# A new order inside each build step of a four-layer GNN kernel: one-hots, weighting, lots and stores

## What is computed

```python
# layer 0
Wh = h @ W + b
sim = dot(Wh[row], Wh[col]) / max(|Wh[row]| * |Wh[col]|, EPS)
base = adj_v * softplus(deg_coeff[0] * deg_v + deg_coeff[1]) * (row != col)
prop_pos = segment_sum((base * relu(sim))[:, None] * Wh[col], row)
prop_neg = segment_sum((base * -relu(-sim))[:, None] * Wh[col], row)
x = x + scale * (coeff[0] * prop_pos + coeff[1] * prop_neg + coeff[2] * Wh)
# layers 1 to 3: LightGCN with three hops, GIN, gated mean over the neighbours
```

## Time and profile before

| what | us |
|---|---|
| median of the three runs | 1067.99 |
| the profiled execution, its own time | 1059.61 |
| its span in the trace | 1057.9 |
| mean granted TensorE clock, share of full | 0.943 |
| VectorE busy | 854.9 (81%) |
| TensorE matmuls busy | 840.5 (79%) |
| ScalarE busy | 619.2 (59%) |
| TensorE busy in the 33.00 us from 500 to 533 us | 26.33 |

### The profile page before, as it was taken

The page is one execution under the profiler, slowest core; times in us unless marked ns, Lnnn a source line. Parts: engine busy times, 40 slices in busy tenths (PEclk is TensorE's granted clock), DMA queues, the critical chain, the costliest instruction groups (busy, mean ns, idle before and its releaser), DMA issues. The chain is left out here.

```text
span 1057.9 us, 33568 instructions
## 1 busy us (share of the span) xinstructions
PE 840.5 (79%) x14240; PEld 593.2 (56%) x14240; DVE 854.9 (81%) x1214; ACT 619.2 (59%) x2090; POOL 175.8 (17%) x364
## 2 busy tenths in 40 slices
PE   0695558878787878878778787744999998999997
PEld 0362435544445545455444554424999998996653
DVE  8986778878888888888888888656666798587896
ACT  0764447767767777677776767617999942112000
POOL 4815711112111121111211112100000000000000
PEclk9987569999999999999999999976999999998999
DMA  9933116566666667666675666759700000783893
GB/s 210 232 115 86 54 41 155 136 151 161 153 139 147 147 165 160 139 147 150 165 157 135 150 144 161 164 159 391 302 2 2 2 2 1 307 310 130 323 388 128
DMA packets 44697, 164.32 MB, mean 155 GB/s; under 512 B 14245, under 2 KB 16375, under 8 KB 40823
## 3 DMA queue, kind: packets, MB, share of 16 engines
q1 hardware_dynamic: 33990, 133.22, 42.6%
q0 software_dynamic: 8288, 27.59, 12.8%
q10 hardware_dynamic: 2256, 1.23, 0.5%
HBM read 78.63 MB, written 63.72 MB: 135 GB/s over the span
## 5 line engine op out<-in xcount | busy, mean ns | idle before, releaser
L1170 PE MATMUL b_ps<-b_mv,b_soh 64*128 64x50 bf16 (+1 forms) x9600 | 192.3, 189 | 119.9 <-DVE b_mv L1055 66.4
L1170 PEld LDWEIGHTS b_ps<-b_mv,b_soh 64*128 64x128 bf16 x9600 | 164.2, 95 | 171.9 <-DVE b_mv L1055 110.9
L1390 PE MATMUL layers_ps<-layers_u,layers_c 128*128 128x192 bf16 x2500 | 210.9, 247 | 11.4 <-ACT layers_u L1572 8.8
L1390 PEld LDWEIGHTS layers_ps<-layers_u,layers_c 128*128 128x128 bf16 x2500 | 208.0, 98 | 16.5 <-DVE layers_y L1696 8.0
L946 ACT ACTIVATE b_c_row<-b_ps 128x300 bf16<-128x300 f32 (+1 forms) x275 | 119.7, 435 | 79.5 <-PE b_ps L1170 72.6
L1093 DVE TENSOR_TENSOR b_y<-b_sim,b_ps 128x512 f32<-128x512 f32 (+1 forms) x175 | 109.9, 628 | 63.9 <-PE b_ps L1224 59.3
L964 ACT ACTIVATE b_pos<-b_ps,k_coef 128x1024 f32<-128x1024 f32 x100 | 92.8, 928 | 91.9 <-PE b_ps L1170 90.7
L1055 DVE TENSOR_TENSOR b_mv<-b_mv,b_parts 128x2808 bf16<-128x2808 bf16 x100 | 145.6, 1456 | 0.0
L1581 ACT ACTIVATE k_passed<-layers_c 128x128 bf16<-128x128 bf16 x450 | 131.4, 294 | 0.0
L1051 DVE TENSOR_TENSOR b_soh<-k_numbers,b_bits 128x2304 bf16<-128x2304 bf16 x100 | 121.9, 1219 | 0.0
L1082 DVE SCALAR_TENSOR_TENSOR b_sim<-b_ps,k_coef,b_pos 128x1024 f32<-128x1024 f32 x100 | 104.6, 1046 | 16.6 <-ACT b_pos L964 16.6
(11 more groups left out here) (275 smaller groups left out, 1123.4 us busy)
## 6 DMA issues: line engine op xcount, KB each, us to landing
layers_c<-g_blocks SPq DMA_DIRECT2D x25, 1600.0 KB, 9.2
g_blocks<-b_g_row SPq DMA_DIRECT2D x52, 400.0 KB
c_blocks<-b_c_row SPq DMA_DIRECT2D x25, 800.0 KB
g_blocks<-head_odd SPq DMA_DIRECT2D x48, 400.0 KB
layers_c<-c_blocks SPq DMA_DIRECT2D x12, 1600.0 KB, 26.3
k_passed<-b_sent POOLq DMA_DIRECT2D x24, 768.0 KB, 6.5
prep_attr<-in_edge_attr SPq DMA_DIRECT2D x2, 1883.0 KB
prep_attr<-in_edge_attr SPq DMA_DIRECT2D x1, 1876.0 KB
```

Of the source, the lines that this page charges most:

```text
L1170: return nc.tensor.matmul(out, lhsT, rhs, start=start, stop=True, skip_group_check=True)
L1390: return nc.tensor.matmul(out_, lhsT, rhs, start=start, stop=True, skip_group_check=True)
```

## The change

The tables get a new order, and ScalarE a table of its own, `AORDER`. In `VORDER` the pair `("hi", o)`, `("hot", o)` becomes three entries: `hi` (line 1048 now), `soh` (line 1051) and `mv` (line 1056), which can stand apart. `soh` now has the waits of `hi`, since it can come first. No instruction is added or taken away inside a step. In SP's loop both halves of the gate sums go two lots earlier.

```diff
-ORDER = [("sims", 0), ("lot", 0), ("turn", 0), ("lot", 1), ("sims", 1), ("turn", 1), ("lot", 2), ("lot", 3), ("turn", 2),
-         ("prop", 0), ("prop", 1), ("sims", 2), ("turn", 3), ("lot", 4), ("lot", 5), ("lot", 6), ("lot", 7), ("turn", 4),
-         ("prop", 2), ("prop", 3), ("sims", 3), ("turn", 5), ("lot", 8), ("lot", 9), ("lot", 10), ("turn", 6), ("prop", 4),
-         ("prop", 5), ("prop", 6)]
+ORDER = [("sims", 0), ("lot", 0), ("turn", 0), ("lot", 1), ("lot", 2), ("sims", 1), ("turn", 1), ("lot", 3), ("lot", 4),
+         ("turn", 2), ("lot", 5), ("prop", 0), ("prop", 1), ("sims", 2), ("turn", 3), ("lot", 6), ("lot", 7), ("turn", 4),
+         ("prop", 2), ("prop", 3), ("sims", 3), ("turn", 5), ("lot", 8), ("lot", 9), ("turn", 6), ("prop", 4), ("prop", 5),
+         ("lot", 10), ("prop", 6)]
-LEAVE = [("lot", 4), ("lot", 8), ("prop", 5), ("prop", 6)]
+VORDER = [("hi", 1), ("soh", 1), ("sim", 0), ("y", 0), ("mv", 1), ("hi", 2), ("y", 1), ("soh", 2), ("sim", 1), ("y", 2),
...
+AORDER = [("sims", 0), ("lot", 0), ("lot", 1), ("lot", 2), ("sims", 1), ("lot", 3), ("lot", 4), ("lot", 5), ("sims", 2),
+          ("send", 0), ("lot", 6), ("lot", 7), ("sims", 3), ("send", 1), ("lot", 8), ("lot", 9), ("send", 2), ("lot", 10),
+          ("send", 3)]
...
-                    sp.wait_ge(s["evac"], 3 * NL * b + 6 + 3 * 4)
+                    sp.wait_ge(s["evac"], 3 * NL * b + 6 + 3 * 2)
                     gated_out(b - 1, 0, 2)
-                    sp.wait_ge(s["evac"], 3 * NL * b + 6 + 3 * 8)
+                    sp.wait_ge(s["evac"], 3 * NL * b + 6 + 3 * 6)
                     gated_out(b - 1, 2, 4)
...
-                if part == "hi":
+                if part != "mv":
                     dve.wait_ge(s["doubled"], 8 * w + (2 * o + 1))
                     dve.wait_ge(s["lot"], NL * w + (ENDS[o - 2] + NL if o >= 2 else ENDS[o + 2]))
```

More of the change, by code:

```diff
@@ L671, in _ @@
                 sp.wait_ge(s_kept, 80)
-ORDER = [("sims", 0), ("lot", 0), ("turn", 0), ("lot", 1), ("sims", 1), ("turn", 1), ("lot", 2), ("lot", 3), ("turn", 2),
-         ("prop", 0), ("prop", 1), ("sims", 2), ("turn", 3), ("lot", 4), ("lot", 5), ("lot", 6), ("lot", 7), ("turn", 4),
-         ("prop", 2), ("prop", 3), ("sims", 3), ("turn", 5), ("lot", 8), ("lot", 9), ("lot", 10), ("turn", 6), ("prop", 4),
-         ("prop", 5), ("prop", 6)]
-VORDER = [("sim", 0), ("y", 0), ("hi", 1), ("hot", 1), ("y", 1), ("sim", 1), ("y", 2), ("hi", 2), ("hot", 2), ("add", 0), ("y", 3),
-          ("sim", 2), ("y", 4), ("hi", 3), ("hot", 3), ("add", 1), ("y", 5), ("hi", 0), ("sim", 3), ("y", 6),
-          ("hot", 0), ("add", 2), ("add", 3)]
-LEAVE = [("lot", 4), ("lot", 8), ("prop", 5), ("prop", 6)]
+ORDER = [("sims", 0), ("lot", 0), ("turn", 0), ("lot", 1), ("lot", 2), ("sims", 1), ("turn", 1), ("lot", 3), ("lot", 4),
[3 more added lines that the diff above has]
+VORDER = [("hi", 1), ("soh", 1), ("sim", 0), ("y", 0), ("mv", 1), ("hi", 2), ("y", 1), ("soh", 2), ("sim", 1), ("y", 2),
+          ("mv", 2), ("soh", 3), ("y", 3), ("add", 0), ("sim", 2), ("y", 4), ("hi", 3), ("mv", 3), ("y", 5), ("add", 1),
+          ("sim", 3), ("soh", 0), ("y", 6), ("hi", 0), ("mv", 0), ("add", 2), ("add", 3)]
+AORDER = [("sims", 0), ("lot", 0), ("lot", 1), ("lot", 2), ("sims", 1), ("lot", 3), ("lot", 4), ("lot", 5), ("sims", 2),
+          ("send", 0), ("lot", 6), ("lot", 7), ("sims", 3), ("send", 1), ("lot", 8), ("lot", 9), ("send", 2), ("lot", 10),
+          ("send", 3)]
 def rounds_of(eng, table):
@@ L987, in step @@
                 begin(r, w, b, par)
-                for what, i in ORDER:
+                for what, i in AORDER:
                     if what == "lot":
@@ L992, in step @@
                         positive(w - 1, i)
[L993 to L996, removed]
+                    if what == "send" and isinstance(w, int) and w <= BYSUM:
+                        send(w - 1, i)
             def end(r):
@@ L1045, in onehots @@
                 hi = halves(mv[b][:, 0:n, 0, :])
-                if part == "hi":
+                if part != "mv":
                     dve.wait_ge(s["doubled"], 8 * w + (2 * o + 1))
                     dve.wait_ge(s["lot"], NL * w + (ENDS[o - 2] + NL if o >= 2 else ENDS[o + 2]))
+                if part == "hi":
                     nc.vector.tensor_tensor(hi, nums(HI), twice(0, HI), ALU.is_equal).then_inc(s["hot"], 1)
                     return
-                nc.vector.tensor_tensor(halves(soh[b][:, 0:n, :]), nums(P), twice(1, P), ALU.is_equal)
+                if part == "soh":
+                    nc.vector.tensor_tensor(halves(soh[b][:, 0:n, :]), nums(P), twice(1, P), ALU.is_equal)
+                    return
                 dve.wait_ge(s["hot"], 4 * w + r + (o + 1))
@@ L1120, in first @@
                 for o in range(4):
-                    onehots(r, r * NB, o, "hi")
-                    onehots(r, r * NB, o, "hot")
+                    for part in ("hi", "soh", "mv"):
+                        onehots(r, r * NB, o, part)
                     if not again(r) and o == 2:
@@ L1127, in first @@
                     count_degrees()
-                onehots(r, r * NB + 1, 0, "hi")
-                onehots(r, r * NB + 1, 0, "hot")
+                for part in ("hi", "soh", "mv"):
+                    onehots(r, r * NB + 1, 0, part)
                 if not again(r):
@@ L1138, in step @@
                 for what, i in VORDER:
-                    if what in ("hi", "hot"):
+                    if what in ("hi", "soh", "mv"):
                         if i:
```

## The result

The changed kernel takes 1021.03 us, the median of four runs (1016.11 to 1027.93), beside 1065.51 for the kernel before on the same chip: a ratio of 0.959 (0.952 to 0.966). A second set of five runs gave 1019.55 beside 1061.28, 0.961 (0.958 to 0.964). Forecast were 1008, within 998 to 1032. The direction and most of the size are right: 60 us off 1068 were forecast, and 44.5 off 1065.5 were measured (42 in the second set). The time is 13 us over the forecast. The profiled execution took 1016.11 us (span 1014.4), where the sum of the terms gave 1001.3, so 14.8 are to be explained.

A forecast was written before the change was run, and what follows sets the result against it. No engine was full; circular waits bounded the step. Savings of 51.8 (steps), 2.3 (irregular intervals), 3.0 (last interval) and 1.2 (end part), sum 58.3, took the profiled 1059.6 to 1001.3; plus 7 for the runs, 1008 us, range 998 to 1032.

The forecast's parts named there:

- The bound and the step: Build steps: VectorE becomes the bound without a wait, 19.71 us a step against 21.96, 2.25 less, 51.8 over 23 intervals.
- y 5 with its 0.25: Tightest place of the hand-played step: y 5 could start at 15.05, VectorE comes to it at 15.3.
- The dependent `mv`: `mv` directly behind the `hi` it reads, groups 3 and 0: 0.17 us each, twice 0.34 a step.
- The irregular intervals: Six longer build intervals, 4.6 us together: half, 2.3, comes back through TensorE's 2.6 us of slack; bounds 0 and 4.6.
- The last interval: Interval into the end, 21.88 us before: TensorE's chain ends it, 18.9 us, 3.0 less.
- The end part: After the last step: turn 4 and its y no longer queue behind the message's add, 1.2 us less, bounds 0 and 2.
- The message: Each step's message, sharing DMA with the earlier stores, lands at 8 to 10 us where it took 6.5, costing nothing.
- slower: the message: Rival: stores make the message late, `sent` of group 0 holds ScalarE and prop 2; landing at 15.5 gives 1082 us; chance 0.04.
- POOL beside VectorE: POOL's copies had run beside a y; now message and four copies fall into `mv`, `hi`, `soh`; no row showed VectorE held.
- The later stages and the level of the runs: Later stages only shift; the runs' median lies 7 us above the profiled execution's 1001.3.
- VectorE still waits, or is held, for some tenths: Rival: handovers or POOL's copies add 0.3 to 1.3 us a step, period 20.0 to 21.0, 1015 to 1038 us; chance 0.25.
- No gain: Rival: an overlooked loop over TensorE and ScalarE keeps the step at 21.9, 1063 to 1068 us; chance 0.05.

The follow-up runs named there:

- the kernel with the message cut: Changed kernel, gate stores at 2 and 6 lots, each step's message cut to 64 of 1536 columns, results incomplete: 995.62 us, ratio 0.9384.
- gates 4 and 8: Changed kernel with the two store halves released at 4 and 8 evacuated lots, as before the change, instead of 2 and 6: 1000.55 us; repeated, 1001.3.
- gates 4 and 7: Changed kernel with the two store halves released at 4 and 7 evacuated lots instead of 2 and 6: 1002.41 us, ratio 0.9435.
- the third order: Changed kernel, new VectorE order with independent instructions between most dependent pairs; store halves at 4 and 8 lots 996.4 us, at 4 and 7 991.88.
- the second run of the changed kernel: The changed kernel once more, unaltered, beside the kernel before at 1061.28 us: 1019.55 us.

## Why the prediction was right or wrong

**The bound and the step: right.** The two orders together free VectorE, and a step without a stop is 19.67 (19.71 in the sum). The hand-played margins held, y 5 with its 0.25 among them: without stops VectorE has no wait at all in the kernel with the message cut. The dependent `mv` was 0.12 instead of 0.17, 0.1 in a step, of which 0.04 are seen. The experiments with one order alone confirm that the waits went round between the engines: 2 and 20 us alone, 62 together.

**The irregular intervals: wrong, 9.1 of the 14.8 us, and the failed step.** I took half of the 4.6 us back, "because TensorE now has 2.6 us of slack". Instead the changed kernel has more of them: 464.70 us for 23 intervals, against the 23 x 19.71 + 2.3 = 455.6 of the sum. The bounds of 0 and 4.6 allowed only a gain. Slack of an engine helps against waits that begin early; the new stops are up to 1.9 us long and stand right ahead of turn 4 and y 4, where VectorE arrives with little to spare. The rows for it had been there: the three short `issue` waits of before and the code queue. I had costed the stores only against the message and ScalarE, not against TensorE's code. With gates 4 and 8, the 24 intervals together take 476.2 us, and the sum had said 455.6 + 18.9 = 474.5. The orders were costed right; it was the third part of the change, the stores, that I costed at nothing and that cost about 20 us.

**The last interval: 2.2 instead of 3.0.** It was 19.71 instead of 18.9. In all three kernels with gates 4 and later that run the changed ORDER and VORDER it is 18.97, so most of this too is the stores' doing (with the message cut it is 19.34).

**The end part: 2.4 us off, the sign wrong.** I had 1.2 less because turn 4 no longer queues behind the add. From the last step's first sim to the first matmul of the layers is 45.6 us, where it was 44.4. The add waits 3.59 for the message and starts 11.66 after the first sim, before 10.28; props 2 and 3 come behind it. What ends the wait there is the DMA, and it ends 1.4 later. In the two runs with gates 4 and 8 and this order the add starts 10.6 and 11.0 after, and the end part takes 44.0 and 43.6: then a part of the 1.2 is there. With gates 4 and 7 it is again 11.8 and 45.6, as in the changed kernel. So the second half of the stores, sooner, goes with a later last message, and I had weighed only turn 4. The end part as a whole follows it only in part: with the third order it is 44.6 at gates 4 and 8 and 43.8 at 4 and 7, though the add starts 10.6 and 11.6 after. That part stays open.

**The message: oversized.** I had it landing 8 to 10 us into the step, 8.5 at least after its start; its median is 7.0 from issue to landing, before 6.5. It holds its place against the stores that come behind it. The rival "slower: the message" rested on the opposite and nothing of it was seen. Others pay: the code of TensorE.

**POOL beside VectorE.** The Trainium skill's page SBUF — State Buffer (section Who interferes with whom, on the shared port pair) says that a VectorE instruction with two SBUF inputs and a GpSimd instruction that reads SBUF exclude each other, and that the one that comes second waits. The trace agrees on POOL's side. A copy of POOL beside `hi` and `soh`, and the same one in the kernel before with VectorE idle:

```profile
149.38 1.12 POOL L808 COPY b_wh_b<-head_whT 128x128 f32<-128x128 f32 x1 [16.35 <-ACT b_fld L932]
```

```profile
148.25 0.29 POOL L808 COPY b_wh_b<-head_whT 128x128 f32<-128x128 f32 x1 [12.89 <-ACT b_fld L932]
```

1.12 against 0.29 us. No row shows VectorE held: the mean of `mv` is 1.62 us before and after, of `soh` 1.35 and 1.36, of `hi` 0.40. The message, which POOL issues, takes 0.5 longer to land, with the stores beside it. My sentence that POOL's copies had run beside a y before was too simple: the mean of this copy was 0.89 already, and is 0.97. And all four kinds of copy together took POOL 133 us before and take 113 now, so the new order did not make POOL's copies dearer as a whole.

**The later stages and the level of the runs.** The layers took 331.6 us, before 330.2; over the kernels of this study they take 330.2 to 334.8, whatever was changed in the build, so 1.4 is within what is not the change's. The first sim came 1.1 late, and stood between 147.0 and 152.8 us over the kernels of this study. Together 9.1 + 0.8 + 2.4 + 1.4 + 1.1 = 14.8. The median lies 4.9 over the profiled execution, where I had 7.

**The rivals.** The time fell into the band of "VectorE still waits, or is held, for some tenths" (1015 to 1038), and its 20.0 to 21.0 per step hold the 20.2. But the mechanism is another: no handover was longer, and POOL held nothing. I had the size and not the cause. "No gain" fell with the steps of 19.67.

**What stays open.** Three steps, those near 370, 410 and 450 us, have a stop with every placing of the stores in the new orders (with the message cut, one of the three, 0.75 us). In all of these kernels the same three blocks of code come due there, 7.1 to 9.3 us into the step, so it is the layout of the code against the step. I saw this in the traces afterwards; no run moved the blocks. What a packet of code waits behind before it starts, the trace doesn't show. In the kernel with gates 4 and 8, all 6 stops between 150 and 640 us come 1.28 to 1.43 us after the end of a packet and at a block start. No run changed the amount of code, so that fewer instructions would take the stops away is not shown.

## What to carry to other kernels

A transfer moved into a free place can make an unbroken stretch with its neighbours. Before moving one, read the DMA share in windows of 2 us and see that a pause is left between them, above all where an engine runs long unrolled code; a wait for `issue` on the fastest engine, however small, is the sign to look for. Where several tables of order belong together, one changed alone says little about all: 2, 20 and 62 us here. And a part of a change that "costs nothing" deserves a run of its own.

## What the chip showed that I had not expected

- TensorE stands still up to 1.9 us (3.2 in the second run of the changed kernel) with no wait when its code is late, and goes on 1.2 to 1.6 us after a 16 KB packet of the queue `instruction` has ended. Each packet is one block of 256 of its instructions, and in the changed kernel no later block had landed yet at any of the 83 block starts looked at. The packets took 0.88 to 1.50 us; those ahead of stops, 0.88 to 0.97, came late because they started late.
- DMA engines full for 10 us, then free for 4, gave no stop in steps of 22 us; full for 12 us, 17 stops in 21 steps of 20.2 us; with a pause of 2 us in it, 6; with the message cut, 4 short ones.
- A dependent VectorE instruction costs 0.12 (`hi` to `mv`) to 0.17 us (sim to y) more than an independent one, and one put between them makes that up: 19.67 to 19.03 us in a step. Over 24 steps that is 15 us, of which 4.9 were measured with gates 4 and 8 (1001.3 to 996.4) and some 11 with gates 4 and 7 (0.9435 to 0.9331).
